# One unrolled program for quantised product and attention: batch outside, head group inside, with the next batch's first stage and the last batch's routing between the heads

## The chip, the core and the metric

The kernel runs on one core of one Trainium2 chip. The metric is the time of the device in microseconds (us), the median of several runs. The profile and the trace come from one further execution. A core has five engines that work beside one another and meet only through semaphores: TensorE (PE, matrix products and transposes), VectorE (DVE), ScalarE (ACT), GpSimd (POOL) and SyncE (SP, which here only issues DMAs). Each engine works through its own instructions in order, so an instruction that waits holds up all behind it on that engine.

## The reference

Four batches of 512 rows, 512 columns wide. Everything is float32 in and out.

```python
x = x + xattn(layernorm(x), ctx)     # both operands rounded to fp8 (e4m3) and scaled back:
                                     # rows in blocks of 128 columns, ctx in blocks of 128 x 128
# then, with hidden = layernorm(x):
h = rmsnorm(hidden, attn_norm_w)
q, k, v = h @ q_w.T, h @ k_w.T, h @ v_w.T           # 16 query heads, 4 key/value heads of 128
q, k = rope(rmsnorm(q)), rope(rmsnorm(k))
hidden = hidden + causal_softmax(q @ k.T / sqrt(128)) @ v @ o_w.T
tok = rmsnorm(hidden, ffn_norm_w)
probs = softmax(tok @ gate_w.T)                     # 8 experts, the best 2 of each row, renormalised
moe = sum over the row's 2 experts e of w_e * (silu(tok @ wg_e.T) * (tok @ wu_e.T)) @ wd_e.T
return x + hidden + moe
```

## The kernel before

The program is five parts, one after another, with a barrier between them (`build`, L76).

**First stage** (`quant_projection`, L103). For each of the four batches it normalises 512 rows (four tiles of 128), finds block maxima, scales, rounds to fp8, transposes, multiplies by the batch's rounded context, adds to x, normalises the sum, applies the attention norm, transposes again, and splits the result in a high and a low part (`hT`), since a float32 product is made of three products of shorter operands (hi*hi, lo*hi, hi*lo: `SPLITS`). Rounding a number to fp8 is done with arithmetic: VectorE makes a magic number of the exponent with a bitwise-and and a max-and-multiply (L356, L357 and their context counterparts), and GpSimd adds and subtracts it (`round_fp8`, L241, L246). ScalarE scales, transposed copies go through PSUM banks, and the batches are pipelined in a loop of three and a last one, so that a batch's parts overlap the next one's. `hT` of every batch, 2 MB, is saved to DRAM. The running sum of a batch stays in SBUF in `acc` (all four batches). The maxima of all four contexts are reduced across partitions by one all-reduce on GpSimd. GpSimd also makes the rotary tables, eight products and a few small instructions (`L273`), after all four batches.

**Attention** (`attention`, L442). There are 16 iterations, it = 4g + b: the head group g (four query heads and one key/value head) outside, the batch b inside. An iteration does, for four heads: scores in four row tiles (`score`, L640), maxima on VectorE (`maxima`, L891), exponentials on ScalarE (`exponentials`, L773), division by the sum on GpSimd (`normalise`, L573) and for the last row tile on VectorE (L905), transposes of the probabilities (`transpose_p`), their hi and lo parts (ScalarE and VectorE), and the product with the values (`values`). Between these, at places `(head, place)` that the table `FILL` (L436) lists, stands the work of other iterations: the projections of the next one (`q`, `kv`, by row tile), its norms (`n`, `m`) and transposes (`t`, `u`), and the output projection of the one before (`o`). All engines read the same table, each takes the kinds that it has a part in, so every queue is written out by hand in one order. At each iteration ScalarE issues a load of the 2 MB `hT` of the next batch into one buffer `hTb` (L749).

The weights of a group are ten chunks of 128 x 512 columns: six of q/k/v, four of the output. They are loaded by SP into a ring of five stages, split in hi (ScalarE, `split_hi`, L752 and L754) and lo (GpSimd, `split_lo`, L552 and L556) in bursts at the end of an iteration: the four output chunks at b = 0, the next group's six q/k/v chunks at b = 2. The columns' norm weight is in `hT` already. The outputs of an iteration are added to `acc` on VectorE (`add_output`, L921).

**Router** (`router`, L988). ScalarE first issues the loads of all eight experts' weights; GpSimd adds each batch's `acc` to the output in DRAM with an accumulating DMA (L1031); then, batch by batch, squares (ScalarE), norm and scaled rows (VectorE, L1085), transposes (PE, L1061), copy (ScalarE), products with the gate (PE, L1070). The rows are saved to DRAM by SP for the gather later, two buffers for four batches.

**Dispatch** (`dispatch`, L1092) computes the lists of rows per expert. SP loads two small tables. **Experts** (`experts`, L1262) works through 39 tiles of 128 rows: a gather on GpSimd, transposes (L1313), products up (L1322), silu, transposes, products down (L1339), and an accumulating scatter to the output. Its first product waits once for all eight experts' weights; each tile's offset in the weights is read from a register.

## Time and profile before

| | |
|---|---|
| median of 3 runs | 1701.13 us (1699.84 to 1703.56) |
| the profiled execution | 1700.5 us, its span 1698.5 |
| mean granted clock of TensorE | 0.887 of full speed |
| busy: TensorE, VectorE, ScalarE, GpSimd | 1287.3, 952.0, 604.7, 501.9 us (76, 56, 36, 30% of the span) |
| DMA | 115.25 MB, mean 68 GB/s |

The page of the profile also cuts the span into 40 equal slices of 42.5 us; each digit is a tenth:

```profile
PE   0221113478998999989999899999845389999996
...
DVE  8979798256775667757767677767422611111110
ACT  1111201245555555555555455555231012222221
POOL 2423150234334333333342433322110023333332
PEclk9995555699999999999999999999955589999998
DMA  6010102312111121111120211100099023333332
```

Slices 1 to 7 are the first stage, 9 to 29 attention, 30 and 31 the router, 32 dispatch, the last eight the experts. [...]

### The profile page before, as it was taken

To read this page: it belongs to the slowest core of one execution; us is meant where nothing else is said; L and a number is where in the kernel's file an instruction comes from. 1 tells how busy PE (TensorE), PEld (TensorE's weight loads), DVE (VectorE), ACT (ScalarE), POOL (GpSimd) and SP (SyncE) were. 2 spreads that over 40 slices of the span, in tenths; PEclk is the share of its full clock that TensorE was granted. 3 is DMA by queue.
4 is the path that set the end of the run, shared out by engine and by line. 5 is a ranking of instruction groups with operands and counts; after the bars stand their busy time and mean duration, and the time that the engine had idled before them with its cause. 6 is when DMAs were issued, how large, how long until landed. Compare 5 with 4: busy or idle time off the path is not lost. (4 is left out here: it accounts for less than half of the span.)

```text
span 1698.5 us, 23301 instructions
## 1 busy us (share of the span) xinstructions
PE 1287.3 (76%) x6606; PEld 981.5 (58%) x6606; DVE 952.0 (56%) x2751; ACT 604.7 (36%) x1969; POOL 501.9 (30%) x635
## 2 busy tenths in 40 slices
PE   0221113478998999989999899999845389999996
PEld 0010101367887878878888788887645056566653
DVE  8979798256775667757767677767422611111110
ACT  1111201245555555555555455555231012222221
POOL 2423150234334333333342433322110023333332
PEclk9995555699999999999999999999955589999998
DMA  6010102312111121111120211100099023333332
GB/s 241 0 75 0 75 0 88 147 51 75 51 51 44 45 76 51 51 38 51 53 74 1 81 51 51 39 14 1 2 371 281 1 50 68 68 63 63 69 67 38
DMA packets 31525, 115.25 MB, mean 68 GB/s; under 512 B 3296, under 2 KB 4064, under 8 KB 27296
## 3 DMA queue, kind: packets, MB, share of 16 engines
q0 software_dynamic: 10848, 24.65, 8.1%
q10 hardware_dynamic: 3744, 51.45, 7.8%
q1 hardware_dynamic: 16800, 37.58, 6.3%
q8 instruction: 59, 0.97, 0.2%
q14 instruction: 74, 0.61, 0.1%
HBM read 82.21 MB, written 31.46 MB: 67 GB/s over the span
## 5 line engine op out<-in xcount | busy, mean ns | idle before, releaser
L623 PE MATMUL bank<-w_hi,hTb 128*128 128x512 f32 (+1 forms) x1024 | 284.9, 352 | 22.6 <-DMA hTb<-hT_scratch 18.4
L775 ACT ACTIVATE prob<-bank,bias,scale 128x128 f32<-128x128 f32 (+3 forms) x256 | 157.2, 616 | 215.8 <-DVE prob L894 215.8
L623 PEld LDWEIGHTS bank<-w_hi,hTb 128*128 128x128 f32 x1024 | 184.1, 193 | 46.4 <-DMA hTb<-hT_scratch 18.8
L576 POOL TENSOR_TENSOR prob<-prob,rtotal 128x128 f32<-128x128 f32 (+2 forms) x192 | 116.6, 616 | 269.4 <-DVE rtotal L900 265.4
L1322 PE MATMUL gu<-we,xT 128*128 x624 | 193.5, 464 | 1.0 <-ACT xT L1366 0.8
L910 DVE TENSOR_TENSOR pT_lo<-bank,pT_hi 128x512 fp32r<-128x512 f32 (+3 forms) x256 | 119.5, 489 | 131.1 <-ACT pT_hi L783 123.0
L623 PE MATMUL bank<-w_lo,hTb 128*128 128x512 f32 (+1 forms) x512 | 174.6, 341 | 0.0
L550 POOL TENSOR_TENSOR r<-r,rot 128x640 f32<-128x640 f32 x64 | 100.0, 1562 | 224.2 <-DVE v_lo L871 224.2
L1322 PEld LDWEIGHTS gu<-we,xT 128*128 128x128 f32 x624 | 116.7, 192 | 60.4 <-issue 3.3
L783 ACT ACTIVATE pT_hi<-bank 128x512 fp32r<-128x512 f32 (+3 forms) x256 | 104.7, 437 | 119.1 <-PE bank L659 119.0
L894 DVE TENSOR_SCALAR_CACHE_REDUCE prob<-bank,nscale 128x128 f32<-128x128 f32 (+3 forms) x256 | 134.8, 545 | 18.2 <-PE bank L650 18.1
L1395 DVE TENSOR_TENSOR hh<-gu,sg 128x352 f32<-128x352 f32 x39 | 20.5, 525 | 192.0 <-ACT sg L1379 192.0
L1300 POOL DMA_INDIRECT out<-y,ids x39 | 61.8, 1586 | 217.6 <-ACT y L1372 213.6
L648 PE MATMUL bank<-kT_hi,qT_hi 128*128 128x128 f32 (+3 forms) x256 | 98.4, 384 | 27.9 <-ACT prob L775 23.2
L1339 PE MATMUL dn<-we,hT 128*128 x234 | 107.0, 593 | 0.7 <-DVE hT L1399 0.7
L659 PE MATMUL bank<-ident,prob 128*128 128x128 f32 x640 | 102.9, 275 | 5.5 <-DVE qT_lo L919 3.8
L690 PE MATMUL bank<-w_hi,aT_hi 128*128 128x512 f32 x256 | 105.0, 410 | 1.5 <-issue 1.5
L297 PE MATMUL part<-cq,xqT 128*128 (+1 forms) x64 | 36.7, 612 | 91.3 <-DVE xs L372 91.0
L623 PEld LDWEIGHTS bank<-w_lo,hTb 128*128 128x128 f32 x512 | 98.7, 193 | 8.8
L690 PE MATMUL bank<-w_hi,aT_lo 128*128 128x512 f32 x256 | 100.5, 392 | 0.0
L690 PE MATMUL bank<-w_lo,aT_hi 128*128 128x512 f32 x256 | 99.8, 390 | 0.0
L672 PE MATMUL bank<-pT_hi,v_hi 128*128 128x512 f32 (+3 forms) x256 | 90.6, 354 | 4.8 <-DVE pT_lo L910 4.8
(222 smaller groups left out, 2755.8 us busy)
## 6 DMA issues: line engine op xcount, KB each, us to landing
hTb<-hT_scratch ACTq DMA_DIRECT2D x16, 2048.0 KB, 8.2
we<-in_wexp ACTq DMA_DIRECT2D x8, 2176.0 KB, 34.4
stage<-in_wqkvo SPq DMA_DIRECT2D x40, 256.0 KB, 3.0
xs<-in_x SPq DMA_DIRECT2D x4, 1024.0 KB, 14.4
cs<-in_ctxT SPq DMA_DIRECT2D x4, 1024.0 KB, 11.3
out<-xs SPq DMA_DIRECT2D x4, 1024.0 KB, 4.5
hT_scratch<-hT_hi SPq DMA_DIRECT2D x4, 1024.0 KB, 3.9
hT_scratch<-hT_lo SPq DMA_DIRECT2D x4, 1024.0 KB, 6.3
```

The source lines that it names most:

```text
L550: nc.gpsimd.tensor_tensor(r[:, t, :], r[:, t, :], rot[t % 2][:, :], ALU.add).then_inc(rope_added, 1)
L576: nc.gpsimd.tensor_tensor(p, p, rtotal[:, 4 * h + q:4 * h + q + 1].broadcast_to([P, KEYS[q]]), ALU.mult).then_inc(prob_ready, 1)
L623: last = nc.tensor.matmul(o, hT[:, a, k, t * P:(t + 1) * P], wkv(c, k) if kv else wq(c, k), start=(k == 0 and n == 0), stop=(k == KC - 1 a ...
L648: nc.tensor.matmul(o[:, 0:KEYS[q]], qT[a][:, h, q * P:(q + 1) * P], kT[b % 2][c][:, 0:KEYS[q]], start=(n == 0), stop=False)
L659: last = nc.tensor.transpose(bank[PT + j % 2][:, (q - j) * P:(q - j + 1) * P], prob[h % 2][:, P_AT[q] + j * P:P_AT[q] + (j + 1) * P], iden ...
L690: last = nc.tensor.matmul(bank[t % 2][:, :], aT[b % 2][a][:, h, t * P:(t + 1) * P], wo(c, h), start=(h == 0 and n == 0), stop=(h == G - 1 ...
L775: nc.scalar.activation(prob[h % 2][:, P_AT[q]:P_AT[q] + KEYS[q]], bank[SC + q % 2][:, 0:KEYS[q]], ACT.Exp, bias=bias[:, 4 * h + q:4 * h + ...
L783: nc.scalar.activation(pT[0][:, PT_AT[j]:PT_AT[j] + QS[j]], bank[PT + j % 2][:, 0:QS[j]], ACT.Copy).then_inc(pt_hi, 1)
L894: nc.vector.tensor_scalar(prob[h % 2][:, P_AT[q]:P_AT[q] + KEYS[q]], bank[SC + q % 2][:, 0:KEYS[q]], nscale[b % 2][:, q, h:h + 1], None, A ...
L910: nc.vector.tensor_tensor(pT[1][:, sl], bank[PT + j % 2][:, 0:QS[j]], pT[0][:, sl].bitcast(F32), ALU.subtract).then_inc(pt_lo, 1)
L1322: last = nc.tensor.matmul(gu[i % 2][u][:, 0:I], xT[i % 2][:, k, :], we[:, bass.ds(at + (k * GU + u * I), I)], start=(k == 0), stop=(k == K ...
L1339: last = nc.tensor.matmul(dn[i % 2][:, :], hT[i % 2][:, c, :], we[:, bass.ds(at + (KC * GU + c * D), D)], start=(c == 0), stop=(c == IC - 1))
```

## The change

First stage, attention and router become one program, `mixer`, and the batch is outside now: iteration it is `b, g = divmod(it, 4)`. Nothing is looped; all sixteen iterations are written out.

- Only batch 0's first stage stands ahead of attention. The first stage of batch b+1 is spread over iterations g = 0, 1, 2 of batch b by a table `FRONT`, and the routing of batch b-1 stands in iteration g = 3 of batch b (`ROUTE`). The last batch's routing follows the last iteration. The table `FILL` stays nearly as it was.
- The context of one batch is in one buffer `cb`; its maxima are all-reduced per batch, the first behind `tables()` on GpSimd's queue. All four instructions of an fp8 rounding are on VectorE. The rounded operands are scaled back to float32 in place, and the product is four float32 matmuls of 128 x 512 per row tile (before: four bf16 products of blocks, scaled and added afterwards).
- `hT` is not saved any more; it is computed once per batch and stays in SBUF. The norm of the hidden rows is kept apart as `r2` and `hms` and enters v and the q/k norms; the column weight is multiplied into the q/k/v weights when they are split.
- A group's weights are split once (hi on ScalarE, lo on VectorE, a ring of three stages): group 0's q/k/v chunks in the first stage, group 1's ahead of iteration 0, groups 2 and 3's in iterations 0 and 1, the output chunks in iterations 1 to 4. They are saved to DRAM (`ws_scratch`), and from then on SP loads the split weights of an iteration, 5 MB, again.
- The sum goes to DRAM (`save_x1`) when a batch's first stage is done; the accumulating DMA with the hidden rows is issued by GpSimd in iteration g = 1 of the next batch. `acc` has three buffers for four batches.
- The experts' weights are loaded by SP in dispatch, with a semaphore for each expert, ahead of the save of the padding row. An expert tile waits for its own expert only, through a register.

The diff, cut to its core:

```diff
+        mixer(nc, x, ctxT, w_attn, wqkvo, qn, kn, cos, sin, w_ffn, gate, ident_d, mask_d, ident, logits, h2_dram, out)
+        dispatch(nc, ranklow_d, disp_d, wexp, we, w_in, logits, idg, ids, wslot, eoff, eneed, out)
+        experts(nc, we, w_in, ident, idg, ids, wslot, eoff, eneed, h2_dram, out)
...
+FILL = {(0, 1): [("u", 4)], (0, 2): [("q", 0)], (0, 3): [("kv", 0), ("q", 1)],
+        (1, 1): [("kv", 1)], (1, 2): [("q", 2)], (1, 3): [("kv", 2)],
+        (2, 1): [("q", 3)], (2, 2): [("kv", 3), ("o", 0)], (2, 3): [("n", 0), ("o", 1)],
+        (3, 1): [("m", 0), ("o", 2)], (3, 2): [("o", 3)], (3, 3): [("t", 0), ("t", 1), ("t", 2), ("t", 3)]}
+FRONT = ({(0, 1): [("cm", 0)], (0, 2): [("cs", 0)], (0, 3): [("cv", 0)],
+          (1, 1): [("cr", 0), ("cv", 1)], (1, 2): [("cd", 0), ("cr", 1), ("cv", 2)], (1, 3): [("cd", 1), ("cr", 2), ("cv", 3)],
+          (2, 1): [("cd", 2), ("cr", 3), ("xb", 0), ("xb", 1)], (2, 2): [("cd", 3), ("xb", 2), ("xb", 3)],
+          (3, 1): [("xn", 0)], (3, 2): [("xh", 0)], (3, 3): [("xh", 1)]},
+         {(0, 1): [("xa", 0)], (0, 2): [("xv", 0), ("xa", 1)], (0, 3): [("xr", 0), ("xv", 1)],
+          (1, 1): [("xd", 0), ("xr", 1)], (1, 2): [("xt", 0), ("xd", 1), ("xh", 2)], (1, 3): [("xp", 0), ("xa", 2)],
+          (2, 1): [("xt", 1), ("xv", 2), ("xh", 3)], (2, 2): [("xp", 1), ("xr", 2), ("xa", 3)], (2, 3): [("xd", 2), ("xv", 3)],
+          (3, 1): [("xt", 2), ("xr", 3)], (3, 2): [("xp", 2), ("xd", 3)]},
+         {(0, 2): [("xt", 3)], (0, 3): [("xp", 3)], (1, 2): [("yn", 0)], (2, 1): [("yh", 0), ("yh", 1), ("yr", 0)],
+          (2, 2): [("yh", 2), ("yh", 3)], (2, 3): [("ht", 0)], (3, 1): [("ht", 1)], (3, 2): [("ht", 2)]},
+         {})
+FRONT_FIRST = ({}, {}, {(3, 3): [("ht", 3)]}, {})
+ROUTE = {(0, 1): [("rs", 0), ("rs", 1)], (0, 2): [("rs", 2), ("rs", 3)], (0, 3): [("rn", 0)],
+         (1, 1): [("rh", 0)], (1, 2): [("rt", 0), ("rh", 1)], (1, 3): [("rl", 0)],
+         (2, 1): [("rt", 1), ("rh", 2)], (2, 2): [("rl", 1)], (2, 3): [("rt", 2), ("rh", 3)],
+         (3, 1): [("rl", 2)], (3, 2): [("rt", 3)]}
+ROUTE_FIRST = {(3, 3): [("rl", 3)]}
+SPLIT_Q = {(3, 1): [("wq", 0), ("wq", 1)], (3, 2): [("wq", 2), ("wq", 3)], (3, 3): [("wq", 4), ("wq", 5)]}
+SPLIT_O = {(1, 1): [("wo", 0)], (1, 2): [("wo", 1)], (1, 3): [("wo", 2)], (2, 1): [("wo", 3)]}
...
+        @block.sync
...
+            def load_split(g, lo, hi, saved, landed):
+                for i in range(2):
+                    sp.wait_ge(saved[i], 16 * HKV)
+                    sp.dma_start(w[i][:, lo:hi, :].rearrange("p c n -> p (c n)").bitcast(F32), ws_dram[g, i, :, lo * CH:hi * CH]).then_inc(landed[i], 16)
+            def load_q(j):
+                sp.wait_ge(projq, TT * j)
+                load_split(j % HKV, 0, KC, q_saved, wq_in)
...
+            for it in range(NIT):
+                b, g = divmod(it, HKV)
...
+                if g == 0 and 1 <= b and b + 1 < B:
+                    load_x(b + 1)
...
+                if g == 2 and b + 1 < B:
+                    save_x1(b + 1)
+                    if b + 2 < B:
+                        load_ctx(b + 2)
+                if 2 <= it <= HKV:
+                    save_o(it - 1)
+                if g == HKV - 1 and b:
+                    save_h2(b - 1)
+                if HKV <= it + 2 < NIT:
+                    load_q(it + 2)
+                    load_kv(it + 2)
+                if it >= HKV:
+                    load_o(it)
...
         @block.gpsimd
...
+            tables()
+            column_maxima(0)
...
+                if g == 1 and b:
+                    add_hidden(b - 1)
...
         @block.tensor
...
+            def product_x(f, t):
+                n = TT * f + t
+                pe.wait_ge(xT_ready, n + 1)
+                pe.wait_ge(cd_ready, KC * (f + 1))
+                for k in range(KC):
+                    last = nc.tensor.matmul(product_bank(n)[:, :], xT[:, k, :], cb[:, k, :], start=(k == 0), stop=(k == KC - 1))
+                last.then_inc(xp_done, 1)
...
         @block.vector
...
+            def round_fp8(z):
+
+                own.chain(nc.vector.tensor_scalar(xm[:, :].bitcast(U32), z.bitcast(U32), EXPONENT_BITS, None, ALU.bitwise_and))
+                own.chain(nc.vector.tensor_scalar(xm[:, :], xm[:, :], FP8_LEAST_NORMAL, None, ALU.max))
+                own.chain(nc.vector.scalar_tensor_tensor(z, xm[:, :], FP8_ROUND, z, ALU.mult, ALU.add))
+                return nc.vector.scalar_tensor_tensor(z, xm[:, :], FP8_ROUND, z, ALU.mult, ALU.subtract)
...
+            def lo_qkv(j, c):
+                n = RAW.index(("q", j, c))
+                dve.wait_ge(wqkv_hi, QKV * j + c + 1)
+                need(dve, q_saved[1] if c < KC else kv_saved[1], 16 * j)
+                for sl, scale_w in pieces(c):
+                    last = nc.vector.scalar_tensor_tensor(w[1][:, c, sl], stage[n % RING_W][:, sl], scale_w, w[0][:, c, sl].bitcast(F32),
+                                                          ALU.mult, ALU.subtract)
+                last.then_inc(wqkv_lo, 1)
...
-def router(nc, wrow_d, gate_d, wexp, acc, ident, we, w_in, logits, h2_dram, out):
...
@@ dispatch
+            for e in range(E):
+                sp.dma_start(we[:, e * ECOLS:(e + 1) * ECOLS], wexp[e]).then_inc(w_in[e], 16)
+            sp.wait_ge(zeroed, 1)
+            sp.dma_start(out[B * S:B * S + P, :], zrow[:, :]).then_inc(pad_saved, 16)
+            sp.wait_ge(pad_saved, 16)
...
@@ experts
-            pe.wait_ge(w_in, 16 * E)
...
+                pe.wait_ge(w_ready, pe.value_load(eneed[0:1, i:i + 1], min_val=1, max_val=E))
```

In the tables, `c` stands for the context (cm maxima, cs scales, cv scaling, cr rounding, cd scaling back, each by chunk of 128 rows), `x` for the rows (xb statistics, xn norm, xh normalised, xa row scales, xv scaling, xr rounding, xd scaling back, xt transposes, xp product and sum), `y` for the norm of the sum, `ht` for the transposed hidden rows, `r` for routing (rs squares, rn norm, rh rows, rt transposes, rl gate products), `wq` and `wo` for a chunk's split.

## Rows read from the trace of the kernel before

**Rows 1.** Windows by stage: us, busy (count) of PE, PEld, DVE, ACT, POOL; PEclk, DMA share, GB/s
```profile
0.00:303.10 303.10, 60.83 (x192) 25.27 (x192) 258.01 (x664) 45.55 (x142) 85.88 (x57) 0.70 0.18 69
303.10:321.40 18.30, 0.00 (x0) 0.00 (x0) 2.16 (x8) 3.87 (x10) 6.15 (x5) 0.50 0.69 271
321.40:355.80 34.40, 22.70 (x112) 19.22 (x112) 12.05 (x36) 9.04 (x48) 10.26 (x18) 0.85 0.24 85
355.80:1229.70 873.90, 831.13 (x4946) 702.67 (x4944) 591.33 (x1804) 456.78 (x1604) 291.32 (x466) 0.98 0.13 44
1229.70:1310.50 80.80, 40.20 (x192) 39.62 (x192) 19.12 (x66) 20.77 (x48) 6.06 (x5) 0.52 0.99 331
1310.50:1358.45 47.95, 13.48 (x35) 4.00 (x35) 26.98 (x94) 0.31 (x1) 2.12 (x6) 0.50 0.06 20
1358.45:1698.54 340.09, 318.97 (x1131) 190.76 (x1131) 42.33 (x80) 68.44 (x118) 100.11 (x78) 0.97 0.34 61
```
**Rows 2.** Windows of two attention iterations, one with a weight split, one undisturbed
```profile
501.80:561.11 59.31, 54.89 (x318) 46.27 (x317) 37.57 (x118) 31.10 (x107) 23.48 (x34) 0.94 0.19 63
672.08:724.93 52.85, 52.03 (x318) 44.31 (x317) 37.56 (x116) 27.94 (x101) 16.13 (x28) 1.00 0.11 41
```
**Rows 3.** Waits of TensorE in 360 to 1220: sum us, count, longest us
```profile
PE bank L648 <- ACT prob L775: 22.4, 27, 3.9
```
**Rows 4.** ScalarE's timeline in a burst of splits: start, duration, [wait before it]
```profile
515.99 0.63 ACT L754 ACTIVATE w_hi<-stage 128x512 fp32r<-128x512 f32 x1 [1.94 <-DMA stage<-in_wqkvo]
```
**Rows 5.** VectorE's timeline in the first stage
```profile
6.47 2.47 DVE L321 BATCH_NORM_STATS2 stats<-xs 128x6 f32<-128x512 f32 x4 [6.47 <-DMA xs<-in_x]
...
10.32 0.16 DVE L72 SCALAR_TENSOR_TENSOR t<-t,var 128x4 f32<-128x4 f32 x1
...
14.22 2.29 DVE L335 TENSOR_REDUCE amax<-xhat 128x16 f32<-128x2048 f32 x1
...
32.91 0.42 DVE L356 TENSOR_SCALAR m<-v 128x512 uint32<-128x512 uint32 x1
33.36 0.43 DVE L357 TENSOR_SCALAR m<-m 128x512 f32<-128x512 f32 x1
...
38.76 4.71 DVE L356 TENSOR_SCALAR m<-v 128x512 uint32<-128x512 uint32 x1
```
**Rows 6.** Costliest lines, whole span: busy us, mean ns | idle before, releaser
```profile
L273 POOL TENSOR_TENSOR tab_q_c<-cos_sb,wrow_q 128x256 f32<-128x256 f32 x2 | 1.4, 722 | 0.1
...
L1085 DVE SCALAR_TENSOR_TENSOR h<-acc,rms,wrow 128x512 f32<-128x512 f32 x16 | 11.0, 747 | 6.6 <-DMA h_scratch<-h 6.5
...
L905 DVE TENSOR_SCALAR prob<-prob,rtotal 128x512 f32<-128x512 f32 x64 | 45.7, 713 | 2.3
```
**Rows 7.** The chain of work that ended last, in the experts: start, length
```profile
1378.89 0.44 PE xtr L1313 x4
1379.33 2.58 PE dn L1339 x6
```
**Rows 8.** TensorE's timeline in the router
```profile
1251.27 1.09 PE L1061 MATMUL tr<-ident,h 128*128 128x128 f32 x4
...
1262.45 1.71 PE L1070 MATMUL pl<-gate,tokT 128*128 128x8 f32 x8
```
**Rows 9.** One line's durations: least, median, most ns; first and last start
```profile
L905 DVE TENSOR_SCALAR prob<-prob,rtotal x64: 485/487/1460, 364.8 to 1209.9; 128x512 f32<-128x512 f32 x64
```
**Rows 10.** GpSimd's timeline, in the first stage and in the router
```profile
38.63 4.56 POOL L246 TENSOR_TENSOR cq<-cv,cm 128x2048 bf16<-128x2048 f32 x1
...
1230.60 5.53 POOL L1031 DMA_DIRECT2D out<-acc  x4
```
**Rows 11.** DMA issues: count, KB each, median us from issue to landing
```profile
hTb<-hT_scratch ACTq DMA_DIRECT2D x16, 2048.0 KB, 8.2
...
we<-in_wexp ACTq DMA_DIRECT2D x8, 2176.0 KB, 34.4
```
**Rows 12.** A window of 10 us in the router, columns as in rows 1
```profile
1250.00:1260.00 10.00, 6.32 (x31) 6.23 (x31) 1.38 (x9) 4.31 (x11) 0.00 (x0) 0.50 1.02 375
```

## What the change does to the time: the prediction

> **What bounds the kernel now.** I read the windows by stage first, then the windows by attention iteration, the waits of TensorE, and last the durations of single lines. The stages [rows 1] follow one another: first stage of all four batches 303.1 us, hand-over 18.3, first projections 34.4, attention 873.9, router 80.8, dispatch 48.0, experts 340.1. Before attention's first scores 355.8 us pass. VectorE is busy 258.0 of the 303.1 us of the first stage and TensorE 60.8; in the router the DMA share is 0.99 and TensorE runs at 0.52 of its clock; in attention TensorE is busy 831 of 874 us. So two stages lie beside an idle TensorE, and the middle is bound by TensorE. An undisturbed attention iteration is 52.85 us: TensorE 52.0, VectorE 37.6, ScalarE 27.9, GpSimd 16.1 [rows 2]. VectorE has 15 us of room, ScalarE 25. Iterations with a weight split are longer, the one shown 59.31 [rows 2]: ScalarE splits six chunks in a row, waits 1.94 us for the sixth's load, and the exponentials stand behind it; the scores' wait for exponentials is 22.4 us over attention, 3.9 the longest [rows 3, 4].
>
> **The sum.** All against this profiled execution: 1700.5 us, span 1698.5; the three runs' median is 1701.1, 0.6 above, which I let go.
>
> *Front.* Only batch 0's first stage stays ahead. VectorE orders it: rows land at 6.5, statistics 2.5, normalisation 14 small instructions at 0.2 each [rows 5]: 12.2. Context maxima 2.3; two row scales of 1.4 (a reduce a quarter as wide as the 2.29 us one, four small ones): 17.3. The context scales wait for GpSimd's all-reduce, which now stands behind `tables()`: eight products of 0.72 us [rows 6] and small ones, after constants issued behind eleven other transfers, to about 22.5. Then 0.9; eight roundings of fp8, each two instructions of 0.45 and two three-operand ones that I put at 0.7 (the nearest, L1085, has a mean of 0.75 in the middle of DMA traffic), 2.3 each [rows 5, 6]: 18.6; two row scales 2.8: 45. The last two row tiles go through dequantise, transposes, copy and product in turn (one `xT`, one at a time): 11 us with the add, 56. Norm of the sum 3.9; the saved x1 lands at about 61; four hidden rows 2.5; four turns of transposes, copy, subtraction at 2.1: 72. The first projections to the first scores are the same code, 34.4 [rows 1]: 106.5. Then group 1's weights are split ahead of iteration 0; chunks 3 to 5 can only be loaded when 0 to 2 leave the ring of three: +5.5. So 112 instead of 355.8, **−244** (102 to 125).
>
> *Attention, what goes.* 40 chunk splits in bursts become splits spread over iterations 0 to 4, and later weights come split from DRAM. Attention's 873.9 us are 28 over sixteen times 52.85; the one long iteration shown has 6.5 of it [rows 2], and with the bursts I take 26 of the 28 as gone. **−26** (−15 to −28). The lo parts move from GpSimd to VectorE, 0.7 us each.
>
> *Attention, what comes, TensorE.* Four transposes 0.44 us, six 512-wide fp32 matmuls 2.58, so 0.43 each [rows 7]. A batch's first stage has 16 transposes before the product, 16 after it and 16 matmuls: 1.8+1.8+6.9 = 10.4 us, three times 31. A routed batch has 16 transposes (1.8) and 16 narrow matmuls: eight 1.71 at half clock [rows 8], so 0.11 each at full clock, 1.7, or 3.4 if nothing of them overlaps: 4 on average, three times 12. TensorE alone makes it +43.
>
> *Attention, what comes, VectorE.* It is the engine that may not have room, since all rounding of fp8 moves onto it (before, GpSimd did the two additions). A rounding costs 2.3 us undisturbed and, by the one SBUF-only instruction that already runs in attention, whose mean is 713 ns against a median of 487 [rows 6, 9], up to 3.4; that one runs right when GpSimd is released, so I take 2.9. In the g=0 iteration come maxima 2.3, scales 0.9, four context roundings 11.6, statistics 2.5, norm 3.2: 20.5, so 58 of VectorE's time, plus about 4 it cannot avoid waiting: 61 to 62. In g=1: row scales 5.8, four roundings 11.6, three adds with statistics 4: 21.5, so 63. In g=2: 10.4 on VectorE, but TensorE 56.7: 58 to 59. In g=3: TensorE +4 and short serial hops where a batch is routed: 58. Over 52.85 that is, for b=0: 11, 17, 6, 1 (iterations 0 and 1 also carry six q/kv chunks each, 4.3 us, 1 to 4 four output chunks each, 2.9); for b=1: 11, 10, 6, 6; b=2: 9, 10, 6, 6; b=3: 0, 0, 0, 4. Together +103, of which TensorE's 43 is part. To it: the output's accumulating DMA is now issued by GpSimd between normalisations, four took 5.53 us [rows 10], so 1.4 for each of three: +4. And stalls of 2 to 3 us in the heavy heads will at times drop the clock, as the split did (granted 0.94 in the 59.31 us iteration [rows 2]): +6. Net attention: −26+103+4+6 = **+87** (+20 to +150).
>
> GpSimd and VectorE: the same bitwise-and took 0.42 us at 32.91 and 4.71 at 38.76, where GpSimd ran one long addition from 38.63 for 4.56 [rows 5, 10]. [...]
>
> *SP's queue.* From iteration 2 on it reloads 5 MB of split weights an iteration instead of 2 MB of hT. A 2 MB load lands in 8.2 us [rows 11]. The q reload is issued once the last q projection is through (half an iteration before its use), in g=3 iterations only behind `save_h2`, which waits for the last routed row: some 14 us remain. I cost it at nothing; without that cover it is up to 8 us each time.
>
> *Router tail.* Three of four batches are routed inside. The last: squares 3.3, norm 2.4, first row 0.75, four serial turns of transposes, copy, gate matmuls, copy at 2.9: **18 instead of 80.8, −63** (15 to 24). The 80.8 were so long because the hidden rows' save waited in a DMA system full of expert weights (share 0.99 [rows 1]).
>
> *Dispatch.* The 17.8 MB of expert weights [rows 11] are now issued here by SP, and the pad row's save behind them on the same queue; the block ends when that lands. At 375 GB/s [rows 12] 18.9 MB (with the tables and the pad row) need 50 us, with start and landing 54 against 48.0: **+6** (0 to +12). The instructions that hid these loads were the router's.
>
> *Experts.* Each tile gets one more register load and a wait. TensorE was busy without a gap in this stage and its sequencer ran ahead: **+1** (0 to +10).
>
> Sum: −244+87−63+6+1 = −213. 1700.5−213 = **1487 us**, with what lies around the span unchanged.
>
> **Rivals.**
> (A) VectorE's additions vanish in its 15 us of room, attention pays TensorE's 43 and loses the 26: +20 instead of +87, **1420**. For it: 37.6 of 52.85. Against it: in g=0 and g=1 VectorE's work alone is above 58. Chance 0.12 for below 1440.
> (B) In-order engines wait on one another. VectorE and ScalarE both get work between the maxima and exponentials; if each heavy head loses 3 us more and the clock drops once in each heavy iteration (6.8 us at half level cost 3.4): 6×(12+3.4) = 92, **1580**. The same time would come of reloaded weights that are late: 12 loads of 8.2 us, 98. Chance 0.17 for 1540 to 1697.
> [...] Chance 0.02.
> (D) The change doesn't do what it says: the order of a queue, SP's most likely, makes each later batch's first stage run in the open again, a third of 303.1−60 each; the gain shrinks to near nothing. 0.01.
>
> My forecast's case, 1440 to 1540, has 0.68. One rule: a difference under 0.2% (3.4 us) is no change. Faster 0.97, same 0.01, slower 0.02. The range for 8 in 10 adds a little at the lower end to that case: 1435 to 1550.
>
> **What would show it.** First scores at about 112 us. A g=0 and a g=1 iteration of 60 to 65 us with VectorE busy above 90%, g=2 and g=3 near 58, the four of the last batch at 53. The wait of scores for exponentials larger than 22 us in spite of the missing splits. No wait for reloaded weights in TensorE's list. From the last output add to dispatch 18 us. Dispatch near 54, ended by the pad row's save. Experts 340. I am wrong in the main step if heavy iterations stay below 58 (A) or exceed 68 (B).

## The result, and the profile after

The changed kernel takes 1638.8 us (median of 4 runs, 1634.8 to 1643.5) against 1702.0 before: ratio 0.963, 95% interval 0.960 to 0.966. I forecast 1487, so the 213 us of gain came out as 63, and the range of 1435 to 1550 missed. The profiled execution took 1639.66 us, its span 1637.8. Of all executions of this document one stands apart, at 2685.5 us against five of 1584.9 to 1591.4 of the same kernel ("the same again" in the table below); its ratio leaves it out.

Windows of the changed kernel by stage: front, attention, last batch's router, dispatch, experts (columns as in [rows 1]).

```profile
0.00:123.40 123.40, 47.70 (x176) 31.49 (x176) 60.64 (x166) 43.95 (x137) 16.16 (x34) 0.90 0.27 94
123.40:1224.30 1100.90, 951.27 (x5282) 776.97 (x5280) 757.64 (x2270) 557.77 (x1886) 260.03 (x438) 0.94 0.26 94
1224.30:1246.50 22.20, 11.88 (x48) 9.99 (x48) 5.47 (x20) 4.95 (x12) 1.30 (x1) 0.53 0.44 94
1246.50:1296.40 49.90, 13.48 (x35) 3.99 (x35) 27.09 (x95) 0.31 (x1) 2.59 (x7) 0.50 0.91 381
1296.40:1637.80 341.40, 318.79 (x1131) 190.63 (x1131) 42.37 (x80) 68.44 (x118) 100.37 (x78) 0.97 0.35 61
```

Beside [rows 1], stage by stage, in us:

| stage | before | after | difference | forecast |
|---|---|---|---|---|
| up to the first scores | 355.8 | 123.4 | -232 | -244 |
| attention | 873.9 | 1100.9 | **+227** | **+87** |
| router | 80.8 | 22.2 | -59 | -63 |
| dispatch | 48.0 | 49.9 | +2 | +6 |
| experts | 340.1 | 341.4 | +1 | +1 |

The four other stages hold within 12 us, each inside its own range. The miss is in attention, 140 us, and there the term's range, up to +150, was missed too. Iteration lengths, from one application of the norms to the next (L887 before, L1033 after; the last reaches to the end of attention):

| batch | g = 0 | g = 1 | g = 2 | g = 3 |
|---|---|---|---|---|
| 0 | 65.4 | 83.4 | 78.1 | 60.6 |
| 1 | 72.5 | 71.9 | 70.8 | 67.9 |
| 2 | 68.7 | 71.5 | 69.4 | 69.1 |
| 3 | 58.4 | 57.5 | 57.4 | 82 |

I had forecast 60 to 65 for the heavy ones, 58 for the middle ones and 53 for the last batch's. The last number catches the eye: an iteration of the last batch has nothing new in it and still takes 57.4, where the undisturbed one of [rows 2] took 52.85. Windows of such an iteration and of one with products (batch 1, g = 1):

```profile
1027.10:1084.50 57.40, 53.05 (x318) 44.55 (x317) 37.45 (x116) 28.29 (x101) 17.45 (x29) 1.00 0.35 111
479.40:551.20 71.80, 63.60 (x348) 50.39 (x347) 53.73 (x169) 40.21 (x136) 17.51 (x29) 0.98 0.29 89
```

The first has the same 318 TensorE rows and 53 us of work at full clock, so 4.4 us of it are idle. The second has TensorE 89% and VectorE 75% busy: neither is full. TensorE's waits in attention, of the changed kernel (us in all, times, longest):

```profile
PE bank L546 <- ACT prob L756: 48.1, 28, 8.5
PE bank L536 <- DVE kT_lo L1065: 17.7, 10, 3.2
PE bank L586 <- DVE rot L1009: 15.4, 10, 1.9
PE bank L586 <- DVE w_lo L970: 14.0, 4, 4.6
PE bank L568 <- DVE pT_lo L1056: 12.4, 9, 3.2
PE bank L586 <- DVE v_lo L1016: 12.2, 14, 0.9
```

The first is the wait of [rows 3], 22.4 before. The four with kT_lo, rot, w_lo and v_lo are new, but for one wait of 1.6 us for kT_lo before. L586 is the output product, L536 the transposes of q and k: both are the places where the table FILL was changed.

Two more rows bear on the terms, the context product's timeline in the first stage (start, duration) and its durations over the whole run (least, median, most ns):

```profile
57.03 3.70 PE L468 MATMUL bank<-cb,xT 128*128 128x512 f32 x8 [0.75 <-ACT xT L682]
```

```profile
L468 PE MATMUL bank<-cb,xT x128: 590/592/1193, 50.2 to 858.8; 128*128 128x512 f32 x128
```

The program has 64 such matmuls, the trace 128 rows. Each of these float32 matmuls leaves two rows, so a row tile's four matmuls are x8 and 3.70 us.

### The profile page after: what moved, and what is told of

Read it like the earlier page. It is cut to its first block and busy times, and to the rows that moved or that the text cites. A ratio compares the mean times of both kernels' runs of the same rounds, so it can differ in the third digit from the quotient of the medians.

```text
span 1637.8 us, 21147 instructions
## 1 busy us (share of the span) xinstructions
PE 1343.1 (82%) x6670; PEld 1013.1 (62%) x6670; DVE 893.2 (55%) x2631; ACT 675.4 (41%) x2153; POOL 380.4 (23%) x558
## 5 line engine op out<-in xcount | busy, mean ns | idle before, releaser
L514 PE MATMUL bank<-w_hi,hT_hi 128*128 128x512 f32 (+1 forms) x512 | 189.1, 369 | 5.7 <-DVE rot L1009 4.3
L385 POOL TENSOR_TENSOR r<-r,rot 128x640 f32<-128x640 f32 x64 | 103.3, 1614 | 368.2 <-DVE v_lo L1016 368.2
L514 PE MATMUL bank<-w_lo,hT_hi 128*128 128x512 f32 (+1 forms) x512 | 177.8, 347 | 0.0
L514 PE MATMUL bank<-w_hi,hT_lo 128*128 128x512 f32 (+1 forms) x512 | 177.4, 346 | 0.0
L586 PE MATMUL bank<-w_hi,aT_hi 128*128 128x512 f32 x256 | 111.9, 437 | 43.2 <-DVE rot L1009 15.4
L546 PE MATMUL bank<-kT_hi,qT_hi 128*128 128x128 f32 (+3 forms) x256 | 103.8, 406 | 48.1 <-ACT prob L756 48.1
L514 PEld LDWEIGHTS bank<-w_hi,hT_hi 128*128 128x128 f32 x512 | 101.8, 199 | 17.9 <-DVE rot L1009 5.7
L514 PEld LDWEIGHTS bank<-w_hi,hT_lo 128*128 128x128 f32 x512 | 100.5, 196 | 12.1
L514 PEld LDWEIGHTS bank<-w_lo,hT_hi 128*128 128x128 f32 x512 | 101.3, 198 | 9.1
L568 PE MATMUL bank<-pT_hi,v_hi 128*128 128x512 f32 (+3 forms) x256 | 96.4, 377 | 12.5 <-DVE pT_lo L1056 12.4
L586 PE MATMUL bank<-w_hi,aT_lo 128*128 128x512 f32 x256 | 105.5, 412 | 0.0
```

The costliest lines, as they stand in the source:

```text
L385: nc.gpsimd.tensor_tensor(r[:, t, :], r[:, t, :], rot[t % 2][:, :], ALU.add).then_inc(rope_added, 1)
L514: last = nc.tensor.matmul(o, hT[a][:, k, t * P:(t + 1) * P], wkv(c, k) if kv else wq(c, k), start=(k == 0 and n == 0), stop=(k == KC - 1 a ...
L546: nc.tensor.matmul(o[:, 0:KEYS[q]], qT[a][:, h, q * P:(q + 1) * P], kT[it % 2][c][:, 0:KEYS[q]], start=(n == 0), stop=False)
L586: last = nc.tensor.matmul(bank[t % 2][:, :], aT[a][:, (G * o + h) % RING_A, t * P:(t + 1) * P], wo(c, h), start=(h == 0 and n == 0), stop= ...
```

## The experiments

Medians in us, and ratios to the kernel before with their 95% intervals. Differences to the changed kernel (1638.8) or to another are of medians. "Both mends" are the first output tile one place later and the fourth transpose in bank 0. "Both cuts" are the quarter product and the short rounding. A probe (extra VectorE work) is work without use that only prices a place.

| kernel | median | ratio | interval |
|---|---|---|---|
| before, with the changed table | 1774.2 | 1.043 | 1.041 to 1.045 |
| changed, first output tile one place later | 1598.7 | 0.939 | 0.938 to 0.941 |
| changed, fourth transpose in bank 0 | 1634.7 | 0.962 | 0.959 to 0.964 |
| changed, both mends | 1596.0 | 0.939 | 0.936 to 0.941 |
| changed, no first stage in attention | 1501.4 | 0.882 | 0.881 to 0.884 |
| changed, quarter product | 1613.4 | 0.949 | 0.946 to 0.952 |
| changed, short rounding | 1605.1 | 0.944 | 0.942 to 0.947 |
| changed, both cuts | 1587.2 | 0.933 | 0.931 to 0.934 |
| before, extra VectorE work in place 1 | 1745.2 | 1.026 | 1.024 to 1.028 |
| the same in place 2 | 1735.0 | 1.019 | 1.017 to 1.021 |
| the same in place 3 | 1822.5 | 1.071 | 1.069 to 1.073 |
| both mends, maxima ahead of the tables | 1587.7 | 0.933 | 0.931 to 0.934 |
| the same again, beside the one below it | 1587.5 | 0.932 | 0.931 to 0.934 |
| rearranged, but the output chunks | 1589.3 | 0.934 | 0.932 to 0.936 |
| rearranged | 1603.9 | 0.942 | 0.940 to 0.944 |
| changed, no reload | 1639.7 | 0.962 | 0.960 to 0.964 |
| changed, copy for the all-reduce | 1628.5 | 0.956 | 0.953 to 0.958 |
| **both mends, all maxima in front** | **1582.0** | 0.929 | 0.927 to 0.931 |

### The output tiles' place

**The kernel before with the changed table** (FILL alone):

```diff
-        (2, 1): [("q", 3)], (2, 2): [("kv", 3)], (2, 3): [("n", 0), ("o", 0)],
-        (3, 1): [("m", 0), ("o", 1)], (3, 2): [("o", 2)], (3, 3): [("t", 0), ("t", 1), ("t", 2), ("o", 3), ("t", 3)]}
+        (2, 1): [("q", 3)], (2, 2): [("kv", 3), ("o", 0)], (2, 3): [("n", 0), ("o", 1)],
+        (3, 1): [("m", 0), ("o", 2)], (3, 2): [("o", 3)], (3, 3): [("t", 0), ("t", 1), ("t", 2), ("t", 3)]}
```

> The kernel before, with the table FILL of the changed kernel and nothing else. Theory 1 (placement): the changed kernel's table costs each iteration the waits that its trace shows (TensorE at L586 1.5 and 0.9 us, at L536 1.6 us, and the restart behind each), 57.45 against 52.85 in iterations that hold nothing new, so 4.6 us for each of 15 iterations: 1701 + 69 = 1770 (1750 to 1780). Theory 2 (engine work): these waits are slack made by VectorE's added work elsewhere; moved alone they cost under 10 us: 1711 at most.

Measured +74 to its own before. Its waits of TensorE in attention:

```profile
PE bank L637 <- DVE kT_lo L919: 24.7, 15, 1.6
PE bank L648 <- ACT prob L775: 19.6, 27, 3.8
PE bank L690 <- DVE rot L865: 19.0, 14, 1.5
PE bank L690 <- DVE v_lo L871: 11.5, 14, 0.8
```

The waits for kT_lo, rot and v_lo are there in a kernel that has nothing else of the change, and its undisturbed iterations are 57.3. Shown: moving the four output tiles one place forward costs 4.5 us in an iteration that holds nothing else, and 74 us in all. In the old place an output tile stood between transposes 2 and 3, and TensorE worked while ScalarE and VectorE made the hi and lo parts that the next step needs. One place after the last `kv` projection it stood clear of the rotation that frees the banks.

**The changed kernel, first output tile one place later:**

```diff
-        (2, 1): [("q", 3)], (2, 2): [("kv", 3), ("o", 0)], (2, 3): [("n", 0), ("o", 1)],
+        (2, 1): [("q", 3)], (2, 2): [("kv", 3)], (2, 3): [("n", 0), ("o", 0), ("o", 1)],
```

> The changed kernel with the first output tile one place later, ('o', 0) in (2, 3) beside ('o', 1). Theory 1: the waits of the output product for the rotation (15.4 us), for v_lo (12.2) and for the output weights' lo part (14.0) go, the transposes' 17.7 stay: 1639 - 28 to 42, so 1597 to 1611. Theory 2: the time comes back at the next wait: over 1630.

Measured -40, inside the 28 to 42 of theory 1. Its waits, where the ones for rot, w_lo and v_lo are gone from the output product:

```profile
PE bank L546 <- ACT prob L756: 46.0, 25, 8.2
PE bank L568 <- DVE pT_lo L1056: 23.4, 14, 3.2
PE bank L536 <- DVE kT_lo L1065: 17.8, 10, 3.2
```

The wait for pT_lo grew by 11, and the time still fell by what theory 1 said. Iterations of the last batch take 54.5 to 55.6 now and not 57.4 to 58.4, so 1.7 us over the 52.85 of [rows 2] are left.

**Fourth transpose to another bank**, alone and with the last edit:

```diff
-        TR = (PT, PT + 1, AUX, PT, AUX)
+        TR = (PT, PT + 1, AUX, 0, AUX)
...
-                if i >= 2:
-                    need(pe, qk_lo, (G + 1) * j + {2: 0, 3: 1, 4: 3}[i])
+                if i in (2, 4):
+                    need(pe, qk_lo, (G + 1) * j + {2: 0, 4: 3}[i])
+                if i == 3:
+                    need(pe, o_added, TT * (j - 2) + 3)
```

> The changed kernel; the transposes of the third head's queries (i = 3) go to the output bank 0, not to the bank that the key's transposes hold. The table stays the changed one. Theory 1 (placement): without an output tile between i = 2 and i = 3 TensorE waits for kT_lo, 17.7 us in all in the changed kernel's trace; this wait goes and 1639 becomes 1621 (1616 to 1626). Rival: the next wait (the first scores of the next iteration for exponentials) takes it up, 1634 or more.

> Both mends: first output tile one place later and the transposes to bank 0. Theory 1: they add up, 1599 - 18 = 1581 (1576 to 1588), and an iteration of the last batch is 53, as before the change. Rival: they share a gap, 1590 or more.

Measured 1634.7 (-4) and 1596.0 (-3 to the kernel with the later output tile). Here theory 1 fell and the rival held. Of the kernel with the bank alone:

```profile
PE bank L548 <- DVE qT_lo L1067: 18.9, 10, 3.3
```

17.7 us of waiting for kT_lo became 18.9 of waiting for qT_lo, by the first scores of the next iteration. So it was no shortage of a bank. That it is the latency of transpose, hi and lo, which the output tile had covered, is argued from this and from the kernel before with the changed table, and no run shows it alone. Putting an output tile there again would need a seventh slot in the ring `aT` (the ring of six lets a head's slot be reused only when the four tiles of the last output are done); that wasn't tried.

### What the first stage costs inside attention

**No first stage in attention** (the change's units left out for batches 1 to 3, with the waits that belong to them):

```diff
-    if b + 1 < B:
-        yield from FRONT_FIRST[g].get(slot, ())
...
-    if b + 1 < B:
-        yield from FRONT[g].get(slot, ())
```

> The changed kernel without the first stages of batches 1 to 3 (their rows of x are still loaded and saved; attention takes the hidden rows of batch 0 for every batch). It prices all that is spread over attention but routing and weight splits. By the iterations of the trace against 57.45: the first stage has 79 us in batches 1 and 2 (15+14+13 and 11+14+12), and of batch 0's 55 some 35, the rest being splits: 1639 - 114 = 1525 (1510 to 1540). If what I forecast for it were true (31 of TensorE plus VectorE's excess, some 80): 1559.

Measured 1501.4: the three first stages cost 137 us, 46 each, more than I expected here and far more than the some 80 in my forecast. Its iterations: 54.2, 62.3, 62.2 and 58.0 in batch 0, 58.0, 57.4, 57.4 and 65.3 in batch 1. So routing costs 7.9 an iteration, 65.3 against 57.4 (I had 5 to 6), and a heavy iteration's excess of 14 us in batch 1 is the first stage's.

**Cutting TensorE's and VectorE's share**, singly and together:

```diff
# TensorE: batches 1 to 3, one column block of four
-                for k in range(KC):
+                for k in range(1 if f else KC):
...
# VectorE: batches 1 to 3, only the last instruction of round_fp8
+                if full:
                     own.chain(nc.vector.tensor_scalar(xm[:, :].bitcast(U32), z.bitcast(U32), EXPONENT_BITS, None, ALU.bitwise_and))
                     own.chain(nc.vector.tensor_scalar(xm[:, :], xm[:, :], FP8_LEAST_NORMAL, None, ALU.max))
                     own.chain(nc.vector.scalar_tensor_tensor(z, xm[:, :], FP8_ROUND, z, ALU.mult, ALU.add))
```

> The changed kernel; the context product of batches 1 to 3 takes only the first of its four column blocks, so 36 float32 products of 128x512 are left out. A row tile's four take 3.70 us in the trace, 0.93 each. If TensorE sets the heavy iterations: 36 x 0.93 = 33 less, 1606. If VectorE or a chain between the engines sets them: under 10 less, over 1629.

> The changed kernel; an fp8 rounding of batches 1 to 3 is only the last of its four VectorE instructions, the other three (about 0.45, 0.45 and 0.6 us) are left out, so 24 x 1.5 = 36 us of VectorE's work inside attention. If VectorE sets the heavy iterations: 36 or more less, at most 1603. If TensorE does, under 12 less; half and half if both share them.

> The changed kernel with both cuts, the context product by three quarters and the fp8 roundings by three of four instructions. Singly they gave 25.4 and 33.7 us. If the engines go in step, the two add up: 59 less, 1580 (1573 to 1587). If each iteration had one engine as its bound, a mixture: cutting both frees more than the sum where either alone only uncovers the other (over 70 less).

Measured 1613.4 (-25 of TensorE's 33), 1605.1 (-34) and 1587.2 (-52). The 36 us of VectorE in my expectation were too few: two of the three instructions take 0.42 and 0.69 us, but the one between them has a mean of 0.89 in attention (rows in the last part on the prediction). Windows from the first to the last application of the norms, in the changed kernel and in the one with short roundings, show 46 us less of VectorE (716.98 and 670.57):

```profile
119.29:1141.96 1022.67, 885.32 (x4934) 722.71 (x4935) 716.98 (x2153) 528.44 (x1807) 251.83 (x425) 0.95 0.27 96
```

```profile
117.76:1106.82 989.06, 870.17 (x4934) 713.05 (x4935) 670.57 (x2079) 528.40 (x1807) 253.99 (x425) 0.97 0.28 99
```

So both cuts give about three quarters of the work back, 34 of 46 and 25 of 33, although VectorE idles a quarter of the time in the iteration shown above. Together they give 52 of the 59 that they gave singly, near to adding up and far from the 70 that a change of bounds would give. That alone would not tell engines that share an iteration from iterations with one bound each, for the cuts fall for the most part into different iterations. The iteration lengths of the four profiled executions, summed over batches 0 to 2, tell more:

| iterations | quarter product | short rounding | both |
|---|---|---|---|
| g = 0 (context roundings) | -1 | -18 | -13 |
| g = 1 (roundings of rows, three of four products) | -10 | -15 | -23 |
| g = 2 (the fourth product) | -12 | 0 | -13 |

In g = 1, where both engines' work is cut, each cut alone shortens the iterations, and both together by nearly the sum. Neither engine alone was the bound there.

**VectorE's idle time, measured by itself.** Into the kernel before, in each head of attention, three chained reductions over the constant table `tab`, behind VectorE's fill of place 1, 2 or 3:

```diff
+            def extra(own):
+                for _ in range(3):
+                    own.chain(nc.vector.tensor_reduce(zm[:, :], tab["q", "c"][:, :, :], AX.X, ALU.max))
...
                     maxima(it, b, h, 2)
                     fill(h, 1, work, first, last)
+                    extra(own)
```

> The kernel before; in each head of attention VectorE runs three more chained instructions of 0.69 us, 2.1 us with their waits, behind its fill of place 1, between the third maxima and the inversion of their sums. VectorE then has 8.5 us more an iteration, 46 of 52.9. If its 15 us of idle time are room (my forecast's reckoning: only what lies above the iteration's length costs): 1701, under 20 more. If the engines go in step through a head, so that work there is added to the iteration: up to 64 x 2.2 = 140 more, 1840; I take over 60 more as this theory's mark.

> The kernel before with the same three instructions a head, behind the fill of place 2, after the fourth maxima and ahead of the last inversion. The early place cost 44 us in all, the late one 121. The last row tile's probabilities are divided behind it, the transposes of the next head wait for those: between the two, 60 to 100 more, if it is the distance to the next thing that another engine waits for that sets the price; 0 to 20 more if only the maxima matter.

> The same three instructions a head, behind the fill of place 3, at the head's end. If room is room, 1701 again. If what counts is the place: the next head's first maxima stand behind it, the exponentials wait for them, and the scores' banks come free later, 60 to 140 more; less than in the early place if TensorE has work in hand there (the values of the last head and the fill of place 3).

| behind the fill of | time | added | of 64 x 2.12 us = 136 |
|---|---|---|---|
| place 1 | 1745.2 | +44 | a third |
| place 2 | 1735.0 | +32 | a quarter |
| place 3 | 1822.5 | +121 | nine tenths |

A window of one iteration with the extra work in place 2, and one in place 3:

```profile
665.00:719.60 54.60, 52.92 (x318) 44.33 (x317) 44.28 (x128) 27.72 (x101) 16.15 (x28) 1.00 0.11 40
```

```profile
665.00:726.50 61.50, 55.56 (x326) 46.62 (x327) 47.90 (x136) 29.88 (x109) 17.30 (x30) 0.99 0.11 40
```

and what TensorE waits for in the kernels with places 1 and 3:

```profile
PE bank L673 <- DVE pT_lo L911: 39.6, 39, 1.5
```

```profile
PE bank L649 <- ACT prob L776: 92.3, 66, 3.9
```

The same 8.5 us of VectorE make the iteration 54.6 or 61.5 long. Behind place 3 stand the next head's first maxima, the exponentials wait for them and TensorE's scores for the exponentials: 92 us against 22 before [rows 3]. I expected the middle place to cost between the other two; it was the cheapest. The two theories that I set against each other were both too simple: room is neither free nor worthless, it depends on what stands behind.

**Rearranging the changed kernel by these prices** (on the kernel with both mends and the maxima ahead of the tables, below):

```diff
-          (1, 1): [("cr", 0), ("cv", 1)], (1, 2): [("cd", 0), ("cr", 1), ("cv", 2)], (1, 3): [("cd", 1), ("cr", 2), ("cv", 3)],
+          (1, 1): [("cr", 0), ("cv", 1)], (1, 2): [("cd", 0), ("cr", 1), ("cv", 2)], (1, 3): [("cd", 1), ("cv", 3)],
...
-SPLIT_O = {(1, 1): [("wo", 0)], (1, 2): [("wo", 1)], (1, 3): [("wo", 2)], (2, 1): [("wo", 3)]}
+SPLIT_O = {(1, 1): [("wo", 0)], (1, 2): [("wo", 1)], (2, 1): [("wo", 2)], (2, 2): [("wo", 3)]}
...
-SPLIT_Q = {(3, 1): [("wq", 0), ("wq", 1)], (3, 2): [("wq", 2), ("wq", 3)], (3, 3): [("wq", 4), ("wq", 5)]}
+SPLIT_Q = {(3, 1): [("wq", 0), ("wq", 1), ("wq", 2)], (3, 2): [("wq", 3), ("wq", 4), ("wq", 5)]}
...
```

Left out of the diff are the later places of the same work and the padding row, which is saved ahead of the experts' weights in dispatch.

> The kernel of both mends and the maxima ahead of the tables (1588), with VectorE's work taken out of the places 3 where it can be (a context rounding in g = 0, two q/k/v chunks in iterations 0 and 1, an output chunk in 1 to 4) and the padding row saved ahead of the experts' weights in dispatch. By the two probes an early place costs 0.7 us and a late one 1.9 us for each 2.1 us of VectorE: three roundings of 2.3 save 4, the chunks 8 x 0.7 of work save 3, and the padding row's 2 us behind the end of dispatch's work: 1588 - 9, 1579 (1574 to 1585). If the places don't matter inside the changed kernel, 1586.

Measured 1603.9, slower by 16. My move of the output chunks had put back a wait that the later output tile had removed:

```profile
PE bank L588 <- DVE w_lo L972: 13.9, 4, 6.6
```

> The rearranged kernel with the output chunks' splits put back to their places. They had been moved to end one place before the first output tile, and the trace shows TensorE waiting 13.9 us for w_lo again: that goes, 1604 - 14 = 1590. If the other moves (roundings and chunks out of the places 3, padding row first) are worth anything, it is under the 1588 of the kernel with the maxima ahead of the tables, at 1582 by the probes' prices; if they are worth nothing, 1586 to 1590.

> The kernel of both mends and the maxima ahead of the tables once more, beside the last one on the same chip: 1588 (1585 to 1591).

Measured 1589.3 without that move, and 1587.5 for the kernel that it is compared with, on the same chip. So the output chunks' move, and with it this wait, explains the 14, and the other moves are worth nothing that can be measured. The probes' prices hold for a probe in every head of the old kernel; they did not carry over to a few units in the changed one. Why is not shown.

### The smaller terms

**The first all-reduce ahead of the tables:**

```diff
-            tables()
             column_maxima(0)
+            tables()
```

> Both mends, and on GpSimd the all-reduce of the first context maxima ahead of the tables. VectorE waits 11.0 us for it in the first stage of the changed kernel's trace, and the tables take 7.0 of GpSimd's time ahead of it: 7 less than with both mends, 1574. Rival: the all-reduce is held up by something else (the trace shows 5.9 us of issue ahead of it), no more than 2 less.

Measured -8.3 to the kernel with both mends, near the 7 expected. (The time of 1574 stood on a forecast for both mends that had missed.)

**No reload** (of each reloaded weight tile only the first 8 columns):

```diff
-                    sp.dma_start(w[i][:, lo:hi, :].rearrange("p c n -> p (c n)").bitcast(F32), ws_dram[g, i, :, lo * CH:hi * CH]).then_inc(landed[i], 16)
+                    sp.dma_start(w[i][:, lo, 0:8].bitcast(F32), ws_dram[g, i, :, lo * CH:lo * CH + 8]).then_inc(landed[i], 16)
```

> The changed kernel; of each reload of split weights from iteration 4 on only the first 8 columns are loaded, so 60 MB of DMA are left out (the later batches use group 3's weights). My forecast costs the reloads at nothing: 1639, within 4. Rival: traffic into SBUF slows the engines' reads, or the weights are late: 1639 - 12 or lower.

Measured 1639.7, no difference: the 60 MB of 12 iterations are hidden, as I had costed them.

**The all-reduces inside attention.** GpSimd's timeline in batch 1's first iteration:

```profile
424.64 0.40 POOL L375 PARTITION_ALL_REDUCE camaxall<-camax  x1 [6.03 <-issue]
432.55 0.82 POOL L404 TENSOR_TENSOR prob<-prob,rtotal 128x384 f32<-128x384 f32 x1 [7.51 <-DVE rtotal L1046]
```

Ahead of 0.4 us of work stand 6.0 of issue, and 7.5 pass before the next ordinary instruction starts. That one's gap is put down to VectorE's `rtotal`, but in the kernel with a copy in the all-reduce's place it starts at once:

```profile
418.31 0.20 POOL L376 COPY camaxall<-camax 128x16 f32<-128x16 f32 x1 [4.18 <-DVE camax L909]
418.47 0.82 POOL L407 TENSOR_TENSOR prob<-prob,rtotal 128x384 f32<-128x384 f32 x1
```

> The changed kernel; the all-reduces of batches 1 to 3 are replaced by a GpSimd copy of the same 16 columns, so the maxima are each partition's own. It leaves the first stage's front as it was and takes only the 6.0 and 7.5 us of GpSimd away, three times. If TensorE waits for it: 1639 - 15 = 1624 (1618 to 1630); if there is slack, 1634 or more.

```diff
-                nc.gpsimd.partition_all_reduce(camaxall[:, :], camax[:, :], P, bass.bass_isa.ReduceOp.max).then_inc(callmax_done, 1)
+                if f:
+                    nc.gpsimd.tensor_copy(camaxall[:, :], camax[:, :]).then_inc(callmax_done, 1)
```

> The kernel with both mends and the maxima ahead of the tables (1588 and 1587), and the context maxima of all four batches taken and all-reduced in the first stage, while VectorE waits for the products there; no all-reduce inside attention. In the changed kernel's trace each all-reduce inside holds GpSimd from 418.6 to 432.6, 6.0 us of issue ahead of 0.4 of work and 7.5 more until the next division of probabilities, three times. If TensorE waits for these divisions: a third to a half of the 14 us each, and VectorE's 2.3 us of maxima: 1587 - 20 = 1567 (1560 to 1574). Rival: the divisions have that slack (TensorE's list names GpSimd with only 5.2 us): 1582 or more.

```diff
+            for f in range(1, B):
+                for k in range(KC):
+                    sp.dma_start(early[f][:, k, :], ctxT[f, k * P:(k + 1) * P, :]).then_inc(e_in[f], 16)
...
-            column_maxima(0)
+            for f in range(B):
+                column_maxima(f)
             tables()
...
                 add_product(0, t)
+                if t < B - 1:
+                    ctx_maxima(t + 1)
```

Measured 1628.5 with the copy (-10) and 1582.0 with all maxima in front (-5.5 to 1587.5). The copy's time lies in the range of the first theory (1618 to 1630), at its slow end, and the maxima in front reach just the 1582 of the rival. So the all-reduces cost something, but three quarters or more of GpSimd's 3 x 14 us away are slack. The second run also takes 3 x 2.3 us of maxima off VectorE, so its 5.5 us are not the all-reduces' alone. The last one is the fastest kernel here that leaves nothing out: 57 us faster than the changed kernel and 120 faster than the one before.

## Why the prediction was wrong

- **What bounds the kernel now, front, router, dispatch, experts, SP's queue**: right. Two stages did lie beside an idle TensorE, and moving them gave 291 us of the 307 that these two terms promised; the reload cost nothing (shown by leaving it out). Of the front's 12 us too many 6 are the all-reduce that ended at 28.8 and not 22.5 (5.9 us of issue ahead of it that I hadn't seen); the rest I put down to row tiles' products that take 3.70 us and not 1.7.
- **The step that failed most: a part of the change that isn't in the sum.** My text calls FILL "nearly as it was", and the sum has no term for it: I costed the move of the output tiles at nothing without a reason, and never named the work that hid the latencies there. It is worth 40 us in the changed kernel by the later output tile (14 of it the wait for w_lo, which meets the chunks of my term "1 to 4 four output chunks each, 2.9"), and some 16 more, an estimate, for the ten waits between the transposes (17.7 us in all), which no run gave back. In the kernel before the whole edit costs 74. It shows in iterations that hold nothing new, so even my forecast of 53 for the last batch fell: 57.4.
- **Mis-sized: the context product.** "six 512-wide fp32 matmuls 2.58, so 0.43 each" in my sum [rows 7] was three matmuls in six rows, 0.86 each. Twelve row tiles at 3.70 and not 1.72 are 24 us more of TensorE; as the run with a quarter of the product gave 25 back for 33 of work, I put them at 18 us of time. The code would have told: the experts' down product has three blocks of rows (`IC`). The router's narrow products fell into the same trap: 64 in the code and 128 rows in the trace, 0.95 us for the eight rows of a row tile at full clock inside attention, so 3.8 a batch, and my upper bound of 3.4 was the nearer one.
- **The wrong rule: an iteration is as long as its busiest engine's work, "58 of VectorE's time, plus about 4".** In batch 1, g = 1, I had 59 of VectorE and 63 in all; VectorE was busy 53.7, TensorE 63.6, and the iteration took 71.8, 8 above the busier of the two. Cutting either engine's work gives most of it back, and cutting both nearly the sum, in g = 1 too, which a single bound cannot do; the probes show 32, 44 or 121 us for the same work in VectorE's "room", by its place. By the run without it, the first stages cost 137 against the some 80 of my sum; product and all-reduce have 18 and 10 of the difference, and the remaining 29 I put down to this rule. That is what is left over, not measured alone, and drops of the clock are in it.
- **Missing: the all-reduce in attention**, 10 us by the copy. Routing, 7.9 for an iteration and not 5 to 6, has a few more, and the last iteration, 82.3 us against 67.9 before, has 14 against my 4 (1.8 of which are FILL's: 69.7 in the kernel before with the changed table).
- The parts don't add exactly, since they come from different kernels: 40 + 16 + 18 + 10 + 29 and some 14 of routing are 127 of the 140, and since the 29 are a remainder, the sum proves nothing about them.
- **The clock** fell more than my +6 allowed: granted 0.94 of full over 1100.9 us against 0.98 over 873.9 [rows 1], and as the low level is half of full (0.50 granted over the 49.9 us of dispatch), 2 x 0.06 x 1100.9 = 132 us at the low level against 2 x 0.02 x 873.9 = 35, from rounded clocks. The traces' own stretches at the low level come to 123 us with TensorE busy in 100, against 27 with 25. The eight rows of a row tile's gate product took 0.95 us at full clock in attention and 1.88 at 0.50 in the last batch's router, twice as long. Half of the 75 more, 37 us, is a bound and not a measurement; it is no term of its own beside those above, whose runs measured it with them. A kernel slower than before, for which I had 0.02, did not come; no iteration of attention was below 0.81.
- **Rival B was nearest**: engines that wait on one another. It had 92 us over my forecast, measured are 152; its chance of 0.17 covered up to 1697, and the result lies inside. Its signs came too: all heavy iterations but one are above 68 us, and the scores' wait for exponentials is 48 us. But that the time falls into its range is in good part luck: 56 us are the output tiles' place, which no rival names, 18 a price misread, and only the 29 left over and the clock are its mechanism. Its other branch, late reloads, did not come.
- **A rounding's price**, 2.9 us in my sum. The least, median and most ns of a rounding's third and fourth instruction, which have two SBUF inputs, and of its second, which has one:

```profile
L892 DVE SCALAR_TENSOR_TENSOR xw<-xm,xw x16: 691/693/694, 30.5 to 832.9; 128x512 f32<-128x512 f32 x16
L892 DVE SCALAR_TENSOR_TENSOR cb<-xm,cb x16: 691/693/693, 35.4 to 741.0; 128x512 f32<-128x512 f32 x16
L893 DVE SCALAR_TENSOR_TENSOR xw<-xm,xw x16: 691/691/694, 31.2 to 833.6; 128x512 f32<-128x512 f32 x16
L893 DVE SCALAR_TENSOR_TENSOR cb<-xm,cb x16: 691/692/693, 36.1 to 741.7; 128x512 f32<-128x512 f32 x16
...
L891 DVE TENSOR_SCALAR xm<-xm x32: 426/427/1684, 30.0 to 832.4; 128x512 f32<-128x512 f32 x32
```

None of the 64 of the first kind was disturbed, but none of them ran beside a GpSimd instruction either. The second instruction did nine times, in each beside GpSimd's addition for the rotation (L385) that had started 0.29 us earlier, and took 1657 to 1684 ns; the other 23 took 426 to 429:

```profile
437.29 1.69 POOL L385 TENSOR_TENSOR r<-r,rot 128x640 f32<-128x640 f32 x1 [1.49 <-DVE v_lo L1016]
```

```profile
437.58 1.68 DVE L891 TENSOR_SCALAR xm<-xm 128x512 f32<-128x512 f32 x1
```

In the kernel with the maxima ahead of the tables (the second run of it) four of the first kind do meet GpSimd, at its table products, and take 1.10 us and not 0.69; the eight table products take 0.79 to 1.18 us there, against 0.72 in the changed kernel, where no rounding runs beside them:

```profile
24.47 1.18 POOL L421 TENSOR_TENSOR tab_q_s<-prob 128x256 f32<-128x256 f32 x1
```

```profile
25.09 1.10 DVE L895 SCALAR_TENSOR_TENSOR cb<-xm,cb 128x512 f32<-128x512 f32 x1
```

The mean of the second instruction inside attention is 893 ns, so a rounding there takes 0.42 + 0.89 + 2 x 0.69 = 2.7 us, near my 2.9. It came out so because in the changed kernel only one of a rounding's four instructions meets GpSimd at length, and that in 9 of 24 roundings.

- **Two slips in the working**, neither of which moves the forecast: 6.5 + 2.5 + 14 x 0.2 for the first norm is 11.8 and not 12.2, and L905 isn't the one SBUF-only instruction in attention before; the application of the norms (L887) reads SBUF alone too.

## What to carry to other kernels

An order written out by hand has slack in it that no busy share shows: here an output tile between two transposes covered a latency. When a change edits such a table, compare it entry by entry and cost each move by what now stands next to what; probe the slack with a dummy instruction at each place before counting idle time as room. And count matmuls in the code, not by the rows of the trace: the context product's 64 left 128.

## What was not expected of the hardware

- In the changed kernel 5.9 to 6.3 us of issue stand ahead of each of GpSimd's four all-reduces, behind ordinary instructions. Behind each of the three in attention the next ordinary instruction starts 7.0 to 7.7 us later. In the front of the kernels that have the all-reduce first the trace shows no issue time ahead of it, only a wait for VectorE's maxima of 14.2 and 14.5 us; a cast and a memset start 0.1 and 0.4 us behind it, and between the memset and the first TENSOR_TENSOR stand 6.9 and 7.4 us of issue. What this time goes into is not shown.
- A float32 matmul of 128x512 left two rows in the trace, with a median of 592 ns, and four such matmuls took 3.70 us at full clock, 0.93 each.
- Nine times in the changed kernel a rounding's bitwise-and (L890) started 0.16 us ahead of GpSimd's L385 and kept its 0.42 us; the next instruction (L891), which started 0.28 to 0.29 us behind L385, took 1.66 to 1.68 us and not 0.43, and lasted until 0.28 to 0.29 us after L385's end. L385 took 1.66 to 1.69 us in these nine, against a median of 1.57 over its 64. At the table products above, both engines' instructions took longer.
